# Graph layer on one core: order of ScalarE's work around the first attention steps, part 4's row sums, and the last BatchNorm statistics

## What is computed

```python
xn = layernorm(x)
xt = (xn @ W).reshape(N, 4, 64)                      # L0_gnn
alpha = softmax(leaky_relu(alpha_l[src] + alpha_r[dst], 0.01), axis=1)
gnn = einsum('nh,nhd->nd', alpha[:N], xt[dst[:N]])   # repeated for the 4 heads

t = relu(batchnorm(qkv_projection(logmap0(proj(xn)))))   # 768 channels, statistics over all tokens
s = pointwise(depthwise(t))                              # groups of 32
t2 = logmap0(proj(expmap0(concat(t, s))))                # needs the norm of each token's row
q, k, v = split(t2); q = relu(q); k = relu(k)
out = (v k^T) q / (sum(v) + 1e-15)                       # per token and group, sequence length 1
mix = proj(expmap0(logmap0(...out) @ w_res + b_res))

x = x + gnn + mix
x = x + layernorm(moe(layernorm(x)) + layernorm(x)) * gamma + beta   # top 2 of 8 experts, GELU
```

## Time and profile before

| | us |
|---|---|
| median of 3 runs | 835.66 |
| lowest, highest run | 833.97, 837.52 |
| the profiled execution, its own time | 833.71 |
| its span, first to last instruction | 831.9 |
| PE busy in the span | 780.0 (94%) |
| PE busy / PEclk, 210 to 212 us | 0.73 of 2.00 / 1.00 |
| PE busy / PEclk, 216 to 218 us | 2.00 of 2.00 / 0.54 |

### The profile page before, as it was taken

The page is one execution under the profiler, slowest core; times in us unless marked ns, Lnnn a source line. Parts: engine busy times, 40 slices in busy tenths (PEclk is TensorE's granted clock), DMA queues, the critical chain, the costliest instruction groups (busy, mean ns, idle before and its releaser), DMA issues. The chain is left out here.

```text
span 831.9 us, 15073 instructions
## 1 busy us (share of the span) xinstructions
PE 780.0 (94%) x5042; PEld 639.1 (77%) x5042; DVE 525.7 (63%) x1480; ACT 424.9 (51%) x963; POOL 384.8 (46%) x601
## 2 busy tenths in 40 slices
PE   5899999999798999999669899999999999999996
PEld 3778888888466666666446788888888888888885
DVE  6863488797578888888988635353535353535345
ACT  2566436889679888888657242323222222223230
POOL 2430878878068888877646502221213131313122
PEclk9999999999999999999979999999999999999999
DMA  9855122222011110211100040000000000000000
GB/s 216 208 146 148 43 57 57 51 57 52 8 50 47 51 59 25 63 45 53 41 10 30 20 126 14 26 13 25 13 25 13 25 12 25 16 23 17 22 20 30
DMA packets 35420, 41.31 MB, mean 50 GB/s; under 512 B 11520, under 2 KB 20696, under 8 KB 35339
## 3 DMA queue, kind: packets, MB, share of 16 engines
q1 hardware_dynamic: 22355, 30.71, 12.9%
q0 software_dynamic: 8000, 6.82, 3.8%
q10 hardware_dynamic: 4984, 2.79, 1.4%
HBM read 25.59 MB, written 14.60 MB: 48 GB/s over the span
## 5 line engine op out<-in xcount | busy, mean ns | idle before, releaser
L926 ACT ACTIVATE Z<-ps,b1s 128x250 f32<-128x250 f32 x200 | 93.5, 469 | 233.1 <-PE ps L1195 233.1
L1208 PE MATMUL ps<-Z 128*125 128x256 f32 x800 | 176.5, 379 | 0.0
L1195 PE MATMUL ps<-Z 128*128 128x250 f32 x800 | 173.3, 374 | 0.4 <-DMA Z<-in_w 0.4
L1208 PEld LDWEIGHTS ps<-Z 128*125 128x125 f32 x800 | 150.1, 188 | 22.3
L1195 PEld LDWEIGHTS ps<-Z 128*128 128x128 f32 x800 | 151.4, 189 | 18.3 <-DMA Z<-in_w 0.6
L988 PE MATMUL ps<-Z,L 128*128 128x250 f32 x600 | 126.9, 373 | 0.0
L655 POOL TENSOR_SCALAR zr<-zmv 125x1 f32<-125x1 f32 x50 | 11.1, 221 | 249.2 <-issue 239.9
L988 PEld LDWEIGHTS ps<-Z,L 128*128 128x128 f32 x600 | 113.6, 189 | 13.2
L1794 DVE TENSOR_TENSOR Z<-ps,L 125x256 f32<-125x256 f32 x50 | 21.2, 424 | 160.2 <-PE ps L1208 159.9
L1110 PE MATMUL ps<-wr,Z 128*125 128x256 f32 x400 | 92.6, 384 | 0.0
L780 ACT ACTIVATE Z<-Z,bn_o,bn_s 128x250 f32<-128x250 f32 x150 | 80.7, 598 | 1.5 <-DVE bn_o L1495 1.5
(11 more groups left out here) (221 smaller groups left out, 1274.0 us busy)
## 6 DMA issues: line engine op xcount, KB each, us to landing
Z<-in_x SPq DMA_DIRECT2D x25, 250.0 KB
out<-Z SPq DMA_DIRECT2D x24, 250.0 KB
xt_table<-L SPq DMA_DIRECT2D x25, 231.0 KB
Z<-in_x SPq DMA_DIRECT2D x1, 2016.0 KB
g_table<-gt SPq DMA_DIRECT2D x25, 62.5 KB
gr<-g_table SPq DMA_DIRECT2D x25, 62.5 KB
Z<-in_x SPq DMA_DIRECT2D x1, 1344.0 KB
Z<-in_w SPq DMA_DIRECT2D x2, 512.0 KB, 3.3
```

The costliest lines, as they stand in the source:

```text
L926: a_.activation(ge[:, b % 2, f, :], ps[:, f % 4, 0:BT], ACT.Gelu, bias=b1s[:, f // NF, f % NF:f % NF + 1]).then_inc(gelu_done.sem, 1)
L1195: last = mm(ps[:, f % 4, 0:BT], w1s[:, f // NF, k, (f % NF) * 128:(f % NF + 1) * 128], h_of(b, k), start=(k == 0), stop=(k == KD - 1))
L1208: last = mm(ps[0:TP, 4 + 2 * (b % 2) + t, 0:D], ge[:, b % 2, f, t * TP:(t + 1) * TP], w2s[:, f // NF, f % NF, :], start=(f == 0), stop=(f ...
```

## The change

Five things, all of order and waits; nothing is computed otherwise.

1. *Part 4 two blocks up.* VectorE takes the row sums of blocks 19 to 24 two blocks per made block, behind `make_h` 10, 11 and 12, then the square of part 4 ahead of `make_h(13)` and its clip ahead of `make_h(14)`. ScalarE's two logarithms of part 4 move from s = 14 to s = 13. TensorE gets nine fillers ahead of turning block 2, in threes and fours behind waits for part 1's row steps.
2. *Last statistics.* For n = 74 VectorE takes the statistics from PSUM, when the product is done; ScalarE's copy of it waits for them.
3. *Block 0.* ScalarE does K's square, K's copy and Q's square of block 0 right behind the second pass, then the last pair's exponential, then the squares of Q and K of block 0 (four chunks), V's relu, the squares of V (two chunks) and V's pointwise square, all ahead of the steps. TensorE does `k_sums_s(0)` ahead of `pointwise_v(0)`, and three fillers behind a wait for the four chunks' squares ahead of `norms(0)`.
4. *Late exponential.* In the steps `late_softmax` stands behind `keep_q`, not ahead of K's square.
5. *Q and K of the last blocks.* Q's relus of blocks 20 to 24 move from steps 19 to 23 to the ends of steps 0, 1 and 2 (2, 2 and 1 blocks: `more_relu`, behind `square_t`). `keep_k` is ScalarE's for all blocks.

```diff
@@ ScalarE, first pass
-                    if s == (4, 8, 14)[i - 2]:
+                    if s == (4, 8, 13)[i - 2]:
@@ ScalarE
             def keep_z(n):
                 act.wait_ge(qkv_done.sem, n + 1)
+                if n == 3 * NB - 1:
+                    act.wait_ge(z_sums.sem, z_sums.count(n))
...
-            edge_softmax(EARLY // 2 - 1)
...
             def keep_k(b):
-                if b >= EARLY_Q:
-                    return
...
-            def square_t(b):
+            def square_t(b, c0=0, c1=NC):
...
+            def more_relu(s):
+                for b in range(EARLY_Q + 2 * s, min(EARLY_Q + 2 * s + 2, NB)):
+                    relu(b, R_Q, relu_q)
...
+            square_s(0, R_K)
+            keep_k(0)
+            square_s(0, R_Q)
+            edge_softmax(EARLY // 2 - 1)
+            square_t(0, 0, 4)
             act.wait_ge(bn_done.sem, bn_done.count(2))
             relu(0, R_V, relu_v)
-            square_t(0)
+            square_t(0, 4, NC)
+            square_s(0, R_V)
...
                 (3, tanh),
-                (0, late_softmax),
-                (0, lambda b: square_s(b, R_K)),
-                (0, keep_k),
-                (0, lambda b: square_s(b, R_Q)),
-                (0, keep_q),
-                (0, ahead(lambda b: relu(b, R_Q, relu_q) if b >= EARLY_Q else None)),
+                (0, later(lambda b: square_s(b, R_K))),
+                (0, later(keep_k)),
+                (0, later(lambda b: square_s(b, R_Q))),
+                (0, keep_q),
+                (0, late_softmax),
...
                 (0, ahead(square_t)),
+                (0, more_relu),
@@ TensorE
             def turn_h(b):
+                if b == PARTS[1][0]:
+                    idle_work(7, 4)
+                    pe.wait_ge(row_dve, ROW_ALL + ROW_CLIP + 2)
+                    idle_work(7, 3)
+                    pe.wait_ge(row_dve, 2 * ROW_ALL - 2)
+                    idle_work(7, 2)
...
             def norms(b):
+                if b == 0:
+                    pe.wait_ge(t_sq_0, 1)
+                if b == 0:
+                    idle_work(7, 3)
...
+                (0, lambda b: None if b else k_sums_s(b)),
                 (0, pointwise_v),
-                (0, k_sums_s),
+                (0, lambda b: k_sums_s(b) if b else None),
@@ VectorE
-                dve.wait_ge(z_kept.sem, n + 1)
+                last = n == 3 * NB - 1
+                if last:
+                    dve.wait_ge(qkv_done.sem, n + 1)
+                else:
+                    dve.wait_ge(z_kept.sem, n + 1)
...
-                (0, keep_k),
```

40 lines of the change are left out of this document (20 added, 20 removed).

## The result

The changed kernel takes **832.93 us** (median of 20 runs, 829.48 to 838.50) against 835.66 before (20 runs, 833.61 to 838.79). The ratio is 0.996, with a 95% interval of 0.9946 to 0.9973: 2.7 us less, between 2.3 and 4.5. The profiled execution took 834.59 us, 1.7 above its median, with a span of 832.1 us. Two runs taken with the experiments, 1036.54 us of before and 1808.08 us of e4_first_pass_before, stand far outside the others and are not in the ratios.

The account below looks back on a forecast made before the run. In the attention steps TensorE, closely followed by ScalarE and VectorE, was taken as bound, waiting 7.8 us for ScalarE's square of V's output. Gains 0.3 + 0.0 + 0.4 + 4.6 = 5.3 us gave 830.4 us, range 827.0 to 834.0.

Parts of the forecast that it names:

- (a): Rival: the clock falls in the first steps and the norm sums double, 1.7 us back, 832.1 us; chance 24%.
- (c): Rival: the exponential's move doesn't give its share, steps 4, 7, 11 and 15 keep 2.1 us, 832.5 us; chance 10%.
- The later steps: Steps 4, 7, 11, 15, 19, 20 and 23: TensorE's waits for V's square go, 4.6 us gained (3.0 to 5.3).
- Steps 0 to 3: Block 0's 2.3 us lead, less what Q's relus cost in the first steps: 0.4 us gained (-0.6 to 1.5).
- a half clock in steps 1 to 3: One of two named signs that the forecast would be wrong; the other, steps 7 to 23 waiting over V's square.
- Block 0: Start of the second pass: norm sums start at 214.15 and run at full clock, block 1's products 2.3 us sooner.
- Pure delay: Block 0: the eleven fillers ahead of V's products fill no wait any more and take 3.5 us.
- The statistics from PSUM: Last statistics: variance 0.6 us sooner, but GpSimd's power still waits behind a gather; worth 0.05 us at most.
- The first pass: Sums of part 4 two blocks up: TensorE's wait moves from block 16 to block 14, 0.3 us gained.
- worth nothing, since that DMA is next however fast TensorE was: Nine fillers at block 2 raise the clock, but ScalarE then waits for the table's DMA: 0.0 us.
- Rival (b), the shared port: VectorE and GpSimd contend for SBUF: 829.2 us if step 4's delay goes, 837.6 if all late steps suffer (slower 6%).

Follow-up runs that it names:

- e4_first_pass_before: The changed kernel with the first pass's edits undone (row sums, logs and nine fillers as before): 833.97 us, ratio 0.9979 against the kernel before.
- e9: The kernel before with the first pass's edits alone (row sums two blocks up, logs at turn 13, nine fillers): 834.41 us, ratio 0.9976.
- e1: The kernel before with only the late exponential moved behind Q's copy: 831.77 us, ratio 0.996.
- e6: The changed kernel with Q's relus late again and the exponential behind V's relu of the next block: 828.53 us, ratio 0.9904 against before.
- e12: The changed kernel measured once more, unaltered: 833.14 us, ratio 0.9956 against before.
- Three single parts: The kernel before with the exponential's move, block 0's part (with the last statistics from PSUM) or the first pass's edits, each alone: 831.77, 833.99 and 834.41 us.
- e5: The changed kernel with Q's relus of the last five blocks back in steps 19 to 23: 827.68 us, ratio 0.9889 against before.
- e7: The changed kernel with Q's relus late again and five fillers, not eleven, ahead of V's products of block 0: 827.96 us, ratio 0.9891 against before.
- e10: The changed kernel with Q's relus late, five fillers, and block 24's relus in step 22, not 23: 827.85 us, ratio 0.9893 against before.

## Why the forecast was right, and where its steps were off

The time, 832.93 us, was in the range of 827.0 to 834.0, and the gain was about half of that forecast, 2.7 us instead of 5.3. The 0.60 that the prediction gave to a time under 831.5 went to the wrong side, and rivals (a) and (c), 832.1 and 832.5, came nearer in number than the forecast. The direction and the later steps were right for the reasons given. That the sum still held by half is in part luck, since its terms missed in both directions.

- **The later steps, 4.6 us forecast.** Right. Excess taken off, N3 to N24 fell by 4.1 to 5.0 us in three profiles, the changed kernel's two and e4's (206.0, 206.1 and 205.3 from 210.3; against e9's 209.7 it is 3.5 to 4.4). All waits for L809's successor are gone from step 4 on, as the text said they would be. But it was the exponential alone that did it: e1 has 4.1 of them. The relus' departure from steps 19 to 23, which I counted as a cause beside it, adds 0.8 at the most.
- **Steps 0 to 3, 0.4 us forecast as a gain.** Wrong; this is the step that failed. From the start of block 0 to N3 the changed kernel took 41.05 and 40.06 us, against 38.88: 1.2 to 2.2 us lost. The step took the slack of steps 2 and 3 and the lead of block 0 as enough to pay for the relus; they were not. Within it, N0 to N1 was forecast at 9.75 us and took 10.04, and N1 to N2 at 10.0, which was 9.98 with the clock up. These were near. Three things were missing. The eleven fillers ran partly at the lower clock (4.22 us, not 3.5), so that N0 came 10.3 us behind the start, not 9.4. Step 3's pair was not covered, 0.37 us. And rival (a) came in one of the two, and in e4: the clock fell where it had put the fall, behind the 2.34 us wait of step 1, and cost 1.0 us where I had priced 1.7. The prediction had named a half clock in steps 1 to 3 as a sign of being wrong.
- **What I compared with.** The larger fault is that I priced the relus against the kernel before, where step 1 already waited 1.42 us for ScalarE, and not against the change without them. One exponential's place removes 1.0 of that wait and block 0's part the clock's fall at the norm sums, so that without the relus N0 to N1 is 8.12 us, not 10.56. The relus then cost 3.4 to 4.5 us, and win 0.8, since the exponential's move had already taken the same waits away in the late steps. The sum hid this: it came out as a small gain.
- **Block 0, 2.3 us forecast at block 1's products.** The reason was right in part. The norm sums ran at the full clock in all ten profiles that have this part and in one of the four that don't; that is worth 1.44 us, since they take 1.89 us and not 1.6. The earlier norm sums (0.7 us) did not come, but for the one execution in which the clock held over the fillers (8.71 us). In the other nine it fell behind TensorE's wait of 2.43 us for K's copy, which the text had seen (K's sums wait until "about 208.15") and for which it had charged no clock. Start to block 1's products: 12.1 us against 13.4, so 1.3 us. "Pure delay" is right for the eleven fillers, but more than half of their delay here is the lower clock: at the full clock they take 2.72 us, against 3.78 to 5.06 otherwise.
- **The statistics from PSUM, nothing.** The power stood behind the gather again, at 208.36, as the text said. Beside this, two statistics from PSUM took 0.75 us and two from SBUF 0.74. By the Trainium skill (VectorE: DVE Perf Modes, section on the TRN2 errata) the fixed cost is 120 cycles against 58, of which I had made 0.065 us; the row shows 0.01. But ScalarE's last copy then stood 0.98 us waiting for the statistics, and K's square and copy, for which TensorE waits those 2.43 us, stand behind it. The text called this wait a real cost and gave it no price. No run has this edit undone by itself, so what it costs or wins is open.
- **The first pass, 0.3 us.** The mechanism was right (one wait moved from block 16 to block 14 and made shorter, 1.47 to 0.98), and 0.5 to 0.7 us of the 1.7 fit it. That the fillers are "worth nothing, since that DMA is next however fast TensorE was" is open: 0.7 us lie at the table's landing, with ranges that overlap, and the rest at a clock that fell less often.
- **Rival (b), the shared port.** It is no reason for a loss here, but e6 shows that step 4's last 1.2 us are VectorE's, in rows of 1.64 and 1.12 us beside GpSimd's additions. The Trainium skill (GPSIMD Engine Reference, table of specifications) states that the two share their way into SBUF and that VectorE's instructions with two SBUF inputs contend. The addition, with two, agrees at 1.12 us; the compare has one, and no run here shows why it was slow as well. V's products also wait a little more than before in steps 8 and 12 (0.27 and 0.20 us, none before) and 13 (0.64 us for 0.3), 0.8 us of what the later steps had won.

Put together, the table gives -1.7 us for the first pass (means of the starts), +1.7 from the start to N3, -3.6 from N3 to N24 with the excess of step 22 in it, +0.4 behind N24 (means of after and e12 against before), together -3.2 us. The medians say -2.7 and -3.0. Since before has one profile here and its pieces scatter by up to 1 us, the agreement is partly chance: the spans of the two profiles of the changed kernel are 832.1 and 831.1 us, against 831.9.

**A version that beats both.** The changed kernel without its early relus: 827.7 us, and with five fillers and block 24's relus a step sooner 827.9, both -1.1% against before. Three single parts (-4.0, -1.7, -1.7) sum to -7.4, and the kernel that has them together measured -8.2. With 6 runs each, these three kernels (e5, e7, e10) can't be told from one another.

## What to carry to other kernels

When two edits cure the same wait, price each against the kernel that has the other; here the second won under 1 us of the 2.5 to 3 that it wins alone, and paid its full 3.4. Work moved "into slack" must be laid against the idle time of the step where it lands, and the steps next to a wait are seldom it. Cut each profile at fixed places and compare the pieces: the best pieces repeat to 0.03 us where totals move by 2 us, and one pair of totals, or one pair of starts, can have the sign wrong. Look in each piece at the waits and the granted clock before calling its excess chance. And when the profile names who ended a wait, compare that one's end with the start behind it.
